# Query tiles between the last key tiles, and row maxima joined four units at a time

## What is computed

```
q = (x @ Wq + bq).reshape(1, B * N, H, hd)
kv = (cond @ Wkv + bkv).reshape(1, -1, 2, H, hd)
q = _fq_sym(q, axis=-1);  k = _fq_sym(k, axis=-1);  v = _fq_sym(v, axis=2)
attn = softmax(q k^T);    attn = _fq_unsigned(attn, axis=-1)
out = attn v;             return out @ Wp + bp
```

## Time and profile before

| | us |
|---|---|
| median of 3 runs | 1810.05 (1808.7 to 1810.61) |
| the profiled execution, its own time | 1810.41 |
| its span, first to last instruction | 1808.6 |
| PE busy | 1703.9 (94%) |
| DVE busy | 1499.0 (83%) |
| ACT busy | 1256.8 (69%) |
| POOL busy | 907.0 (50%) |

### The profile page before, as it was taken

One profiled execution on the slowest core, in us unless ns is written; L12 is line 12 of the kernel. 1 busy time (PEld: TensorE's weight loads), 2 busy tenths in 40 slices (PEclk: granted clock), 3 DMA queues, 4 the chain that ended last, 5 costly groups with the idle time before them and its releaser, 6 DMA issues.

```text
span 1808.6 us, 30394 instructions
## 1 busy us (share of the span) xinstructions
PE 1703.9 (94%) x10706; PEld 744.6 (41%) x10706; DVE 1499.0 (83%) x2796; ACT 1256.8 (69%) x2111; POOL 907.0 (50%) x927
## 2 busy tenths in 40 slices
PE   4999999889999999989999999999999998999999
PEld 1332323234444444434444444444444444444444
DVE  6899999877767669787999999999999998883332
ACT  5888888455554442333799999999999996774433
POOL 6567666256445430000488888888888884000000
PEclk9999999989999999999999999999999999999999
DMA  9866651301011005556666666666666567112020
GB/s 222 222 149 134 156 137 42 117 3 24 1 24 44 20 1 168 100 105 124 115 111 107 107 110 105 114 112 113 117 112 109 105 110 240 24 24 47 24 47 24
DMA packets 420631, 170.45 MB, mean 94 GB/s; under 512 B 382080, under 2 KB 391296, under 8 KB 419328
## 3 DMA queue, kind: packets, MB, share of 16 engines
q1 hardware_dynamic: 420480, 168.51, 45.5%
HBM read 69.89 MB, written 4.19 MB: 41 GB/s over the span
## 4 chain that ended last, share of the span: by engine, by line
PE 67%; DVE 19%; ACT 5%; issue 5%; POOL 2%; DMA 1%; SPq 0%; DVEq 0%; ACTq 0%; POOLq 0%
PE a_psM L1541 12%; PE a_psS L1589 9%; PE g_psY L1075 7%; PE g_psG L1062 7%; PE t_psD L2052 6%; DVE rmax L627 5%; PE t_psU L2039 5%; PE a_psO L1601 4%; PE k_psA L1459 3%; PE psO L762 3%; PE psE L765 2%; DVE maxima L1555 2%; ACT a_prob L1677 2%; POOL a_wide L1657 2%; DVE rinv L368 1%
## 5 line engine op out<-in xcount | busy, mean ns | idle before, releaser
L1555 DVE TENSOR_REDUCE maxima<-a_psM 128x1 f32<-128x512 f32 x1024 | 623.4, 681 | 1.9 <-PE a_psM L1541 0.2
L1677 ACT ACTIVATE a_prob<-a_psS,maxima,q_scale 128x1024 uint8<-128x1024 f32 x512 | 610.8, 1210 | 17.0 <-PE a_psS L1589 14.7
L1657 POOL CAST a_wide<-a_pairs 128x2048 int16<-128x2048 uint8 x256 | 484.0, 1900 | 98.0 <-DMA a_pairs<-a_prob 89.9
L1541 PE MATMUL a_psM<-KT,QO 128*128 128x512 bf16 x1024 | 367.5, 383 | 5.2 <-DVE k_kn L1382 1.6
L1589 PE MATMUL a_psS<-KT,QO 128*128 128x512 bf16 x1024 | 305.7, 380 | 3.1 <-ACT a_prob L1677 3.1
L1601 PEld LDWEIGHTS a_psO<-V,a_wide 128*128 128x128 f16 x4096 | 175.2, 96 | 140.5 <-DVE QO L1630 23.0
L1601 PE MATMUL a_psO<-V,a_wide 128*128 128x32 bf16 x4096 | 181.3, 177 | 16.4 <-DVE QO L1630 15.6
L905 DVE SCALAR_TENSOR_TENSOR g_sum<-g_psG,gu_scale,g_sum 128x512 f32<-128x512 f32 x176 | 124.1, 745 | 86.4 <-PE g_psG L1062 71.2
L884 POOL TENSOR_TENSOR g_sum<-g_sum 128x512 f32<-128x512 f32 x88 | 125.8, 1430 | 128.7 <-DVE g_sum L905 128.7
L563 ACT ACTIVATE prob<-psT 128x512 f32<-128x512 f32 x256 | 143.1, 599 | 60.7 <-PE psT L750 60.2
L1010 ACT ACTIVATE g_sum<-g_psG,gu_scale 128x512 f32<-128x512 f32 x176 | 111.5, 682 | 103.8 <-PE g_psG L1062 102.9
(11 more groups left out here) (219 smaller groups left out, 2755.1 us busy)
## 6 DMA issues: line engine op xcount, KB each, us to landing
xs<-in_x SPq DMA_DIRECT2D x64, 256.0 KB, 6.9
cs<-in_ctx SPq DMA_DIRECT2D x64, 256.0 KB, 8.9
KT<-in_w SPq DMA_DIRECT2D x2, 4096.0 KB, 19.1
raw_gu<-in_gu SPq DMA_DIRECT2D x4, 1408.0 KB, 8.6
vs<-in_ctxT SPq DMA_DIRECT2D x16, 256.0 KB, 3.0
a_pairs<-a_prob SPq DMA_TRANSPOSE x256, 3.0
out<-x_sb SPq DMA_DIRECT2D x16, 256.0 KB, 2.6
x_sb<-in_x SPq DMA_DIRECT2D x1, 3584.0 KB, 14.4
```

The costliest lines, as they stand in the source:

```text
L1541: pe.matmul(psM[n % NM][:, :], QOf[:, i * P:(i + 1) * P], KTf[:, keys:keys + 512], start=True, stop=True).then_inc(shown, 1)
L1555: v.reduce_max(tops[i // JOIN % NB][:, i % JOIN, c:c + 1], psM[n % NM][:, :], AX.X).then_inc(topped, 1)
L1657: pool.tensor_copy(wide[i % NV][:, :, :, :].rearrange("p k c q -> p k (c q)"), both).then_inc(widened, 1)
L1677: act.activation(prob[i % NP][:, k * HK:(k + 1) * HK], psS[g % NS][:, :], ACT.Exp, scale=q_scale[:, i:i + 1], bias=bias[i // JOIN % NB][:, ...
```

## The change

- `ORDER` is dealt anew from k8 on: k8 q0 k9 v12 k10 q1 k11 v13 k12 q2 k13 q3 k14 v14 q4 k15 v15, then q5 to q15. The rows of x and their transposes move to the tile `early`, with four buffers of rows; query tiles use `parts` by their turn among keys and queries (`TURN`), and SP waits where a query tile overwrites loaded weights and context.
- DVE normalises the rows of the first four query tiles after v10 (`X_ROWS`); PE turns the first two after k8 (`X_TURNS`), and ACT copies them after its part of k8. The groups of values are rounded after k3, k4, q4 and q5 (`WHOLE`).
- `AHEAD` goes from 4 to 8 and `JOIN` from 2 to 4; `offset` of a join follows `widen` of every fourth unit.
- 32 pieces in place of 16 are dealt to q6 to q15: 3 for each tile and 4 for q10 and q15.

```diff
-        env["maxima"] = sb("maxima", [P, 28], F32)
+        env["maxima"] = sb("maxima", [P, 56], F32)
...
-    NA, AHEAD, FIRST_SHOWN = 3, 4, 8
+    NA, AHEAD, FIRST_SHOWN = 3, 4, 6
+    SHOWN = [32 * max(0, t - FIRST_SHOWN) // (NT - FIRST_SHOWN) for t in range(NT + 1)]
...
-        wkv = words[:, 0:2 * CH * DM].rearrange("p (c n) -> p c n", c=CH)
-        vT = [words[:, 2 * CH * DM + i * TOK:2 * CH * DM + (i + 1) * TOK] for i in range(2)]
-        cT = words[:, 2 * CH * DM + 2 * TOK:].rearrange("p (c n) -> p c n", c=CH)
+        wkv = words[:, 4 * TOK:4 * TOK + 2 * CH * DM].rearrange("p (c n) -> p c n", c=CH)
+        vT = [words[:, (6 + i) * TOK:(7 + i) * TOK] for i in range(2)]
+        cT = [words[:, n * TOK:(n + 1) * TOK].rearrange("p (c n) -> p c n", c=CH) for n in range(1, NTC)]
...
-        xn = [vT[0][:, 0:DM], vT[0][:, DM:2 * DM]] + [khat, rest] * (NT // 2 - 1)
-        xT = [m.rearrange("p (c n) -> p c n", n=P) for m in halves]
+        xn = [early[:, i * DM:(i + 1) * DM] for i in range(4)]
+        xT = [early[:, (4 + i) * DM:(5 + i) * DM].rearrange("p (c n) -> p c n", n=P) for i in range(2)]
...
-        for i in range(NU - AHEAD):
+        for i in range(8):
             ORDER += [("k", i), ("v", AHEAD + i)]
-        ORDER += [("k", t) for t in range(NU - AHEAD, NT)] + [("q", t) for t in range(NT)]
+        ORDER += [("k", 8), ("q", 0), ("k", 9), ("v", 12), ("k", 10), ("q", 1), ("k", 11), ("v", 13), ("k", 12),
+                  ("q", 2), ("k", 13), ("q", 3), ("k", 14), ("v", 14), ("q", 4), ("k", 15), ("v", 15)]
+        ORDER += [("q", t) for t in range(5, NT)]
         SLOT = {item: s for s, item in enumerate(ORDER)}
+        TURNS = [item for item in ORDER if item[0] != "v"]
+        TURN = {item: g for g, item in enumerate(TURNS)}
+        WHOLE = {("k", 3): (0,), ("k", 4): (1,), ("q", 4): (2,), ("q", 5): (3,)}
+        X_ROWS, X_TURNS = ("v", 10), ("k", 8)
+        def all_turned(b, g):
+            return turned[b], 16 * ((g - b) // 2 + 1)
+        def row_turned(t):
+            return all_turned(TURN["q", t] % 2, TURN["q", t])
+        env["keys_done"] = dict(turned=turned, row=row_turned, values=(v_turned, 16 * CH), read=(q_read, NT),
+                                xT=(xT_ready, NT))
...
             def turn_queries(t):
-                if t == 0:
-                    sp.wait_ge(k_done, NT)
+                b = TURN["q", t] % 2
+                if t in (2, 4, 6):
+                    sp.wait_ge(v_done, NU - 6 + t)
+                    sp.wait_ge(k_done, 2 * t + 4)
+                if t == 6:
                     sp.wait_ge(v_ready, CH)
...
             for kind, i in ORDER:
-                if kind == "v" and UNITS[i][1] == NTC - 1:
-                    turn_values(UNITS[i][0])
+                for c in WHOLE.get((kind, i), ()):
+                    turn_values(c)
...
-                free(act, t)
+                free(act, TURN["k", t])
...
                 if t == 0:
-                    act.wait_ge(v_turned, 16 * CH)
+                    act.wait_ge(v_done, NU // 2)
                 if t >= 2:
...
                     keys(i)
-                    if i + AHEAD - 1 in LAST:
-                        whole(LAST.index(i + AHEAD - 1))
-                    if i == NT - 2:
-                        transposed(0)
-                        transposed(1)
                 if kind == "q":
-                    queries(i)
                     if i + 2 < NT:
                         transposed(i + 2)
+                    queries(i)
+                for c in WHOLE.get((kind, i), ()):
+                    whole(c)
+                if (kind, i) == X_TURNS:
+                    transposed(0)
+                    transposed(1)
...
-                free(v, t)
-                v.tensor_tensor(parts[t % 2][:, :, 2, :], by_head(rest[:, :]), high_half(rest[:, :]),
+                free(v, TURN["k", t])
+                v.tensor_tensor(parts[TURN["k", t] % 2][:, :, 2, :], by_head(rest[:, :]), high_half(rest[:, :]),
...
+                if t == 0:
+                    v.wait_ge(v_done, 10)
+                    v.wait_ge(k_done, TPC)
                 if t >= 4:
-                    v.wait_ge(x_turned, t - 1)
-                v.tensor_scalar(xn[t][:, :], x_sb[:, t, :], mv[:, t, 0:1], rstd[:, t:t + 1],
+                    v.wait_ge(x_turned, t - 3)
+                v.tensor_scalar(xn[t % 4][:, :], x_sb[:, t, :], mv[:, t, 0:1], rstd[:, t:t + 1],
                                 ALU.subtract, ALU.mult).then_inc(xn_ready, 1)
...
+                if (kind, i) == X_ROWS:
+                    for t in range(4):
+                        normalise(t)
                 if kind == "k":
-                    if i == NT - 2:
-                        v.wait_ge(v_ready, CH)
-                        normalise(0)
-                        normalise(1)
                     keys(i)
-                    if i == NT - 1:
-                        v.wait_ge(high_ready, 2 * NT)
-                        v.wait_ge(lo_ready, NT)
-                        normalise(2)
-                        normalise(3)
                     if i >= FIRST_SHOWN:
-                        for n in (2 * (i - FIRST_SHOWN), 2 * (i - FIRST_SHOWN) + 1):
+                        for n in range(SHOWN[i], SHOWN[i + 1]):
                             piece(v, n // CH, n % CH)
...
                     keys(i)
-                    if i == NT - 2:
-                        transpose(0)
-                        transpose(1)
+                if (kind, i) == X_TURNS:
+                    transpose(0)
+                    transpose(1)
                 if kind == "q":
...
                     if i == FIRST_SHOWN:
-                        pe.wait_ge(turned[0], 16 * (NT // 2 + 1))
-                        pe.wait_ge(turned[1], 16 * NT // 2)
+                        for b in range(2):
+                            pe.wait_ge(*all_turned(b, TURN["k", NT - 1]))
                     if i >= FIRST_SHOWN:
-                        for n in (2 * (i - FIRST_SHOWN), 2 * (i - FIRST_SHOWN) + 1):
+                        for n in range(SHOWN[i], SHOWN[i + 1]):
                             show(pe, n // CH, n % CH)
...
     NM, NS, NP, NW, NV, NB = 3, 2, 3, 3, 3, 2
-    AHEAD, LAG, JOIN = 4, 4, 2
+    AHEAD, LAG, JOIN = 8, 4, 4
...
-        tops = [maxima[:, 8 * i:8 * i + 8].rearrange("p (a b) -> p a b", b=PIECES) for i in range(NB)]
-        top, low, bias = ([maxima[:, at + 2 * i:at + 2 * i + 2] for i in range(NB)] for at in (16, 20, 24))
+        tops = [maxima[:, 16 * i:16 * i + 16].rearrange("p (a b) -> p a b", b=PIECES) for i in range(NB)]
+        top, low, bias = ([maxima[:, at + JOIN * i:at + JOIN * (i + 1)] for i in range(NB)] for at in (32, 40, 48))
...
-                            pe.wait_ge(keys_done["turned"][t % 2], 16 * (NT // 2 + t // 2 + 1))
+                            pe.wait_ge(*keys_done["row"](t))
...
                 widen(i)
-                if i % JOIN == 0 and i // JOIN + 2 < N // JOIN:
-                    offset(i // JOIN + 2)
+                if i % JOIN == 2 and (i + 6) // JOIN < N // JOIN:
+                    offset((i + 6) // JOIN)
...
-    nc = bacc.Bacc("TRN2", target_bir_lowering=False, num_devices=1, dynamic_dma_scratch_size=2048)
+    nc = bacc.Bacc("TRN2", target_bir_lowering=False, num_devices=1, dynamic_dma_scratch_size=1024)
```

More of the change, by code:

```diff
@@ L1160, in keys_values_queries @@
             "xn", "x_turned", "xT", "q_done", "q_read", "row", "copied"))
-        env["keys_done"] = dict(turned=turned, values=(v_turned, 16 * CH), read=(q_read, NT), xT=(xT_ready, NT))
         heads = (P, H1, D1)
@@ L1165, in keys_values_queries @@
         ORDER = [("v", u) for u in range(AHEAD)]
-        for i in range(NU - AHEAD):
+        for i in range(8):
             ORDER += [("k", i), ("v", AHEAD + i)]
-        ORDER += [("k", t) for t in range(NU - AHEAD, NT)] + [("q", t) for t in range(NT)]
+        ORDER += [("k", 8), ("q", 0), ("k", 9), ("v", 12), ("k", 10), ("q", 1), ("k", 11), ("v", 13), ("k", 12),
+                  ("q", 2), ("k", 13), ("q", 3), ("k", 14), ("v", 14), ("q", 4), ("k", 15), ("v", 15)]
+        ORDER += [("q", t) for t in range(5, NT)]
         SLOT = {item: s for s, item in enumerate(ORDER)}
+        TURNS = [item for item in ORDER if item[0] != "v"]
[8 more added lines that the diff above has]
+                                xT=(xT_ready, NT))
         def context(n):
-            return c_first if n == 0 else cT[:, :, n * TC:(n + 1) * TC]
+            return c_first if n == 0 else cT[n - 1]
         def values_weight(c, i):
@@ L1210, in turn_keys @@
             def turn_keys(t):
+                b = TURN["k", t] % 2
                 sp.wait_ge(high_ready, 2 * t + 2)
@@ L1213, in turn_keys @@
                 sp.dma_start_transpose(KT[:, :, t * P:(t + 1) * P].bitcast(I16),
-                                       parts[t % 2][:, :, :, :].rearrange("p h k d -> p (h k d)").bitcast(I16)
-                                       ).then_inc(turned[t % 2], 16)
```

(18 more changed lines are left out.)

## The result

The changed kernel takes 1813.15 us (median of 12 runs, 1811.28 to 1815.2) beside 1808.35 for the kernel before (12 runs): ratio 1.0025, 95% interval 1.0017 to 1.0032, so 4.5 us slower, between 3.1 and 5.8. Forecast were +2.7 and 1812.7. The profiled execution took 1814.01 with a span of 1812.2, 3.6 more than the span of before.

A forecast was written before the change was run, and what follows sets the result against it. VectorE was taken to bound the attention, TensorE the stretch before it and ScalarE the last units. +5.6 - 12.3 + 9.4 = +2.7 us on the median of 1810.05 gave 1812.7, range 1810.5 to 1815.5.

The forecast's parts named there:

- Part 1: Up to q15's product, on TensorE: old pauses gone, new pauses before q0 and in q10, more shows; +5.6 us.
- The terms of the clock: TensorE's slow clock behind the new pauses: 1.9 us behind the one before q0, 1.5 behind the one in q10.
- the first two terms: Before the attention, on TensorE: old pauses and slow clock gone, -8.8 us; new pause before q0, +5.5, its clock +1.9.
- Part 2: From q15's product to the last maximum, on VectorE: fewer pieces, -8.4 us, and fewer but wider joins, -3.9; sum -12.3.
- Part 3: Last units, on ScalarE: eight instead of four are left when the last maximum is taken, +9.4 us.
- Rival A: Attention: ScalarE becomes the bound in place of VectorE, 3 us more, 1815.7; chance 0.09.
- B: Before the attention: the clock doesn't fall behind the two new pauses, 1.9 and 1.5 us drop out, 1809.3; chance 0.15.
- C: Before q0: no pause, because ScalarE reaches the copies earlier; 7.4 us less, 1805.3; chance 0.07.
- D: Attention's end: ScalarE's last units overlap with the last maxima, VectorE's 12.3 us count in full, 1803.3; chance 0.04.
- E: Mixed key and query tiles stall each other through psA, some 5 us lost again, 1817.7; chance 0.05.
- F: Attention's end: POOL's casts, slowed beside VectorE's additions, set the end; 1 us more, 1813.7; chance 0.04.
- the old pause: TensorE's 5.57 us wait after k14 for VectorE to normalise x; forecast to reappear before q0 at 5.5 us.

The follow-up runs named there:

- turned_at_k7: Kernel after with x's first tiles normalised after v9 and turned after k7, one key tile earlier: 1805.12 us, ratio 0.9976 to the kernel before.
- three_each: Kernel after with the 32 pieces dealt as two to q5 and three to each of q6 to q15: 1809.78 us, ratio 1.0004 to the kernel before.
- order_k7: Kernel before with the new order alone and x's tiles 0 and 1 turned after k7: 1800.15 us; timed again (order_k7_again) 1800.70.
- attend_only: Kernel before, old order, with AHEAD 8, JOIN 4 and 32 pieces dealt to q6 to q15: 1813.43 us, ratio 1.0025 to the kernel before.
- join2_ahead8: Kernel after with two units a join instead of four and four buffers of maxima: 1817.21 us, ratio 1.0035 to the kernel before.
- order_only: Kernel before with the new order of keys, values and queries alone, AHEAD 4 and JOIN 2 kept: 1808.63 us, ratio 0.9997 to the kernel before.
- ahead5_k7: ahead6_k7 with five units ahead, 20 dealt pieces and offset placed after another unit: 1812.7 us, ratio 1.0016 to the kernel before.
- filled_pause: Kernel after with eleven extra fp32 products in the pause before q0: 1813.21 us, ratio 1.0012 to the kernel before.
- filled_just: Kernel after with six extra fp32 products in the pause before q0: 1810.67 us, ratio 1.0006 to the kernel before.
- ahead6_k7: Kernel after with six units ahead, 24 dealt pieces and x's tiles 0 and 1 turned after k7: 1800.03 us; timed again 1797.69.

## Why the prediction held, and where it was off

- **Part 1**, forecast +5.6, measured +6.1. Pauses of 5.64 and 2.56 stand where 5.5 and 2.5 were forecast, and turned_at_k7 and three_each remove them one at a time. Term by term: order_k7 has the 14 shows of before and no pause, so the kernel before lost 9.3 to its pauses (135.1 less 125.8), not 8.8; the pause before q0 costs 7.9 with its clock, not 7.4; the one in q10 costs 4.4 with its clock (turned_at_k7 less order_k7 less 3.0 for 14 shows), not 4.0. The terms of the clock were small, 2.3 and 1.7 in place of 1.9 and 1.5, and each pause was priced at its idle time, without the 0.17 of overlap. That the errors of the first two terms cancel is luck. That the pauses would be followed by the lower level was right here, but of the second it is no rule (below).
- **Part 2**, forecast -12.3, measured -12.6. The shift of 0.08 for the join of 16 numbers, taken from between two bounds, is the row at 1207.10. attend_only has -12.2 and join2_ahead8 gives the joins' part by itself, 3.7 where 3.9 was worked out.
- **Part 3**, forecast +9.4, measured +10.0; order_only and order_k7_again keep 8.6, six units have 13.3, eight 18.6. Behind the last join ScalarE starts 8 halves in before, 10 in ahead5_k7, 12 in ahead6_k7 and 16 in the kernel after, 1.18 apart: `AHEAD` is paid there in full. The 0.6 too little is mostly where the first of these halves stands: 0.28 us behind the join in before (row below), 0.78 in the kernel after (1493.13, 0.20 of it a wait for a transpose of `a_prob`); the other 0.1 is in a few halves 1.19 to 1.23 apart.

```profile
1499.05 1.20 ACT L1677 ACTIVATE a_prob<-a_psS,maxima,q_scale 128x1024 uint8<-128x1024 f32 x1
```

- **The sum** was +2.7, the stages say +3.5 and the ratio +4.5 (3.1 to 5.8). The mechanism was right and the size 1 to 2 us low. By the stages part 1 was 0.5 and the tail 0.6 too small, and part 2's saving 0.3 too small, which is 0.8 together; the ratio's further 1.0 is within its interval. The median lies in the range, but the difference is just over the 0.2% that was taken as no change, so the outcome is "slower", which had the chance 0.34 and not the 0.55.
- **Rival A** falls: in the stretch 895 to 1480 us VectorE waits for nothing, in join2_ahead8 more joins cost their full price, and ScalarE's waits for `score` stay (11.2 us in 13 times; before 12.2 in 14). **B, C and D** fall with the two slow stretches, the pause of 5.64 and the tail of 18.6. **E**: no pause between q0 and q10.
- **F** is right in kind and costs nothing. After the last join:

```profile
1493.08 4.19 POOL L1675 CAST a_wide<-a_pairs 128x2048 int16<-128x2048 uint8 x2 [2.57 <-DMA a_pairs<-a_prob]
1497.23 0.63 POOL L1662 TENSOR_TENSOR maxima<-maxima,q_scale 128x4 f32<-128x4 f32 x1
...
1498.29 9.70 POOL L1675 CAST a_wide<-a_pairs 128x2048 int16<-128x2048 uint8 x5
...
1493.26 4.54 DVE L1844 TENSOR_TENSOR early<-QO,e_sum 128x512 f32<-128x512 f32 x2
```

Two casts take 4.19 us beside VectorE's `early` products of two inputs, and a multiplication 0.63 that takes 0.20 elsewhere; five casts that mostly follow take 9.70. At 2.36 us of ScalarE's work to a unit POOL keeps up: ScalarE shows no wait behind 1493.13, and the rest of the span is as long as before. The addition of 1.51 us that F puts into rows 5 stands at 1498.85 in the trace of before, beside a cast; in the kernel after it takes 0.19 at 1492.44, where no cast runs. This is again what the Trainium skill, GPSIMD Engine Reference, section Specifications, says of shared SBUF interfaces; the page gives no size, these rows do.

What the prediction left lying is its own sentence that the old pause "is moved, not removed": one key tile earlier it is removed, and that is worth 7.9 us, more than twice the loss of 3.5 by the stages.

## What to carry to other kernels

Units shown ahead are paid at the end of the stage, once each at the following engine's pace, and earned back only in work moved off the bound; count both before going deeper. A pause that depends on where a step stands in another engine's list can often be had back by moving that step by one item, and it brings the slow clock's cost with it. Before a waiting instruction is placed in a queue, look at what stands behind it: there the wait costs, not where the waited value is used.

## What the runs showed of the hardware

**The same pause, two outcomes.** Behind the pause of 2.56 or 2.57 us in q10 (with the same work of TensorE before it from q1 on, but for attend_only, which has the old order), the next eight records took 5.29, 5.29, 5.29 and 4.85 us (after, turned_at_k7, join2_ahead8, attend_only), and 3.60 in filled_pause and filled_just. What decides it is open. For a sum the cost is therefore between 0 and 1.7 us. Behind the pause of 5.63 or 5.64 us before q0 the clock fell every time, and the eight records took 5.34, 5.67, 5.91 and 6.07 us (three_each, order_only, after, join2_ahead8): 1.7 to 2.5 us.

**The clock also fell without such a pause.** TensorE in the kernel after, in order of time:

```profile
1492.98 0.60 PE L1607 MATMUL a_psS<-KT,QO 128*128 128x512 bf16 x2 [0.39 <-ACT a_prob L1695]
1493.42 0.35 PE L1619 MATMUL a_psO<-V,a_wide 128*128 128x32 bf16 x8
1494.48 0.60 PE L1607 MATMUL a_psS<-KT,QO 128*128 128x512 bf16 x2 [0.70 <-ACT a_prob L1695]
...
1496.85 1.03 PE L1607 MATMUL a_psS<-KT,QO 128*128 128x512 bf16 x2 [0.16 <-ACT a_prob L1695]
```

and in windows (stretch, its length, busy time of PE, PEld, DVE, ACT and POOL with counts, granted clock, DMA share, GB/s), the kernel after and then filled_pause:

```profile
1492.00:1496.00 4.00, 2.63 (x32) 1.41 (x31) 3.86 (x7) 3.80 (x7) 2.92 (x2) 0.99 0.77 130
1496.00:1500.00 4.00, 3.73 (x32) 1.56 (x30) 3.90 (x5) 4.00 (x7) 3.77 (x4) 0.58 0.53 117
```

```profile
1492.00:1496.00 4.00, 2.83 (x40) 1.70 (x38) 3.93 (x4) 4.00 (x7) 3.75 (x4) 1.00 0.69 119
1496.00:1500.00 4.00, 2.52 (x35) 1.41 (x31) 3.96 (x3) 4.00 (x9) 4.00 (x3) 1.00 0.58 131
```

With no pause over 0.70 us but a third of the time idle (in filled_pause it is 29% and then 37%, and the clock stays up), two `score` products take 1.03 instead of 0.60. It costs under 0.1 us there, since ScalarE is the bound. It isn't always free: in join2_ahead8 the clock is at the lower level too, `score` takes 1.01, and two halves follow 1.35 and 1.62 us behind the one before. The first of them starts right behind such a `score`; for the second the trace shows no releaser.

```profile
1500.00:1503.00 3.00, 3.00 (x30) 1.24 (x29) 2.93 (x4) 2.62 (x5) 2.85 (x4) 0.50 0.39 87
```

turned_at_k7 and three_each have slow `score` products in this stage as well; filled_pause, filled_just, attend_only and order_only have none. What decides it is open.

**The head scatters.** At the end of the head the 14 profiled executions differ by 5 us (734.0 to 739.0), more than the effect in question; two executions of one kernel, on two chips, differ by 2.5 (order_k7) and 3.1 (ahead6_k7), and two kernels on one chip by 4.7. That the spans of before and after could be compared at all is due to their heads, 736.3 and 736.4; comparing stages takes this scatter out.
